# Two chunks interleaved at every second head, and four PSUM banks evacuated one by one, in an attention + FFN kernel on eight cores

## The reference

```python
x = x + layernorm(attention(layernorm(x)))
x = x + layernorm(ffn(layernorm(x)))

# attention, 16 heads of 64, linear, causal, in chunks
q, k, v = split(x @ w_qkv.T + b_qkv)
qf, kf = features(q), features(k)   # normalise, project, square, exp, clip
kv_cum = cumsum(kf * v) + carry ; k_cum = cumsum(kf) + carry
out = (qf . kv_cum) / max(qf . k_cum, 1e-6) @ w_out.T + b_out

# ffn: block diagonal up projection per head (4) and rail (64), then a dense one
y = einsum('btri,hrij->bthrj', x.reshape(b, t, 64, 16), rail_maker)
z = einsum('bthrj,hrkj->bthrk', y, rail_up_proj)
out = gelu(z.reshape(b, t, 16384)) @ w_cproj.T
```

## Time and profile before

| | |
|---|---|
| two runs, median | 4231.64 us (4229.14 and 4234.13) |
| the profiled execution | 4233.17 us |
| its span on the slowest core (core 6) | 4231.6 us |
| spans of the eight cores | 4181.5 to 4231.6 us |
| PE busy | 2215.4 us (52%) |
| DVE busy | 902.6 us (21%) |
| ACT busy | 943.3 us (22%) |
| granted TensorE clock, mean | 0.716 of full speed |
| main chunks of attention | about 799 to 2168 us |
| FFN, from its first layernorm | about 2240 us to the end |

### The profile page before, as it was taken

How to read it: one execution, slowest core, us unless ns; L and a number is a source line. 1 busy time by engine, 2 the same in 40 slices (tenths; PEclk the granted TensorE clock), 3 DMA queues, 4 the chain that set the end, 5 groups by cost and what they waited for, 6 DMA issues and landing times.

```text
span 4231.6 us, 30294 instructions; the slowest of 8 cores (4181.5 to 4231.6 us)
## 1 busy us (share of the span) xinstructions
PE 2215.4 (52%) x10260; PEld 1005.3 (24%) x10368; DVE 902.6 (21%) x1526; ACT 943.3 (22%) x1313; POOL 51.5 (1%) x73
## 2 busy tenths in 40 slices
PE   0334334444445444445445666667762866666664
PEld 0222222222222322223121222222221222222222
DVE  0222222233333233332343000000005100000003
ACT  0222323322322233232202111111102211111111
POOL 1000000000000000000000000000000000000000
PEclk9666666666656666666556788888885888888887
DMA  8000000000000000000002222211223022222221
GB/s 168 5 5 10 5 10 1 1 0 0 1 0 1 0 1 0 0 1 1 0 7 40 40 40 40 34 31 23 33 40 80 1 40 40 40 40 40 40 40 40
DMA packets 55077, 99.55 MB, mean 24 GB/s; under 512 B 2368, under 2 KB 18880, under 8 KB 53824
## 3 DMA queue, kind: packets, MB, share of 16 engines
q0 software_dynamic: 44880, 80.82, 12.1%
q1 hardware_dynamic: 10048, 16.79, 1.3%
HBM read 170.03 MB, written 8.39 MB: 42 GB/s over the span
## 4 chain that ended last, share of the span: by engine, by line
PE 48%; DVE 19%; ACT 12%; DMA 12%; issue 7%; DVEq 1%; ACTq 1%; POOL 0%; SPq 0%; POOLq 0%
PE psB L803 24%; DMA wc<-wcT 9%; PE psA L396 6%; PE psA L766 4%; PE psA L429 3%; DVE oacc L821 3%; DVE railsM L528 2%; DMA xa_bf<-x_carry 2%; DVE pn_bf L346 1%; DVE f32s L319 1%; PE psA L272 1%; PE psB L601 1%; PE psA L339 1%; ACT qk_bf L406 1%; ACT f32s L323 1%
## 5 line engine op out<-in xcount | busy, mean ns | idle before, releaser
L803 PE MATMUL psB<-hsl,wc 128*128 128x512 bf16 x4004 | 1048.5, 405 | 566.3 <-DMA wc<-wcT 439.0
L803 PEld LDWEIGHTS psB<-hsl,wc 128*128 128x128 bf16 x4096 | 376.5, 102 | 1105.7 <-issue 782.4
L777 ACT ACTIVATE hsl<-psA 128x512 bf16<-128x512 f32 x512 | 305.7, 597 | 1360.2 <-PE psA L766 1356.0
L821 DVE TENSOR_TENSOR oacc<-oacc,psB 128x2048 f32<-128x2048 f32 x56 | 128.1, 2288 | 1446.6 <-PE psB L803 1446.6
L396 PE MATMUL psA<-ln_bf,wqkv_bf 128*128 128x256 bf16 x1536 | 248.6, 339 | 84.5 <-DVEq L83 56.3
L266 PE MATMUL psA<-xa_bf,allones_bf 128*128 128x256 bf16 x256 | 58.3, 406 | 371.6 <-DMA xa_bf<-x_carry 211.0
L766 PE MATMUL psA<-ln,railsM 32*128 32x512 bf16 x512 | 210.1, 413 | 24.5 <-DVEq L83 13.8
L396 PEld LDWEIGHTS psA<-ln_bf,wqkv_bf 128*128 128x128 bf16 x1536 | 182.8, 121 | 146.5 <-issue 92.0
L339 PE MATMUL psA<-qk_bf,omega_bf 64*64 64x256 bf16 x384 | 50.9, 412 | 211.5 <-DVEq L83 211.5
L262 ACT ACTIVATE sq_bf<-xa_bf 128x2048 bf16<-128x2048 bf16 x32 | 61.1, 1909 | 443.2 <-DVEq L83 284.2
L429 PE MATMUL psA<-wqkv_bf,ln_bf 128*128 128x512 bf16 x496 | 137.4, 439 | 38.8 <-ACTq L83 20.6
(11 more groups left out here) (150 smaller groups left out, 2028.7 us busy)
## 6 DMA issues: line engine op xcount, KB each, us to landing
wc<-wcT POOLq DMA_DIRECT2D x32, 2048.0 KB, 17.9
x_sb<-x_own SPq DMA_DIRECT2D x8, 1024.0 KB, 23.6
y_out<-oacc SPq DMA_DIRECT2D x8, 1024.0 KB, 4.4
wqkv_bf<-wqkvT POOLq DMA_DIRECT2D x8, 768.0 KB, 47.9
xa_bf<-x_carry POOLq DMA_DIRECT2D x8, 512.0 KB, 5.9
wout_bf<-woutT POOLq DMA_DIRECT2D x8, 256.0 KB, 67.1
rut_bf<-rut POOLq DMA_DIRECT2D x4, 128.0 KB, 5.7
omega_bf<-omega POOLq DMA_DIRECT2D x2, 128.0 KB, 15.3
```

The source lines that it names most:

```text
L777: A_((lambda a, fcl=fcl, zsl=zsl, hb=hb: a.activation(hb[:, fcl * 512:(fcl + 1) * 512], psA[:, zsl * 512:(zsl + 1) * 512], AF.Gelu)), wait ...
L803: t.matmul(psB[:, ob * 512:(ob + 1) * 512], wcbufs[fcl // 8][:, (fcl % 8) * 1024 + obi * 128: (fcl % 8) * 1024 + (obi + 1) * 128], hb[:, f ...
L821: V_((lambda v, g=g, obg=obg: v.tensor_tensor(AP(oacc, obg * 4096 + g * 512, [[8 * 1024, 128], [1024, 4], [1, 512]]), AP(oacc, obg * 4096 ...
```

## The change

Two edits. In stage B, `pump()` is called at every second head instead of every third: 8 times in the head loop instead of 6. In the FFN, the evacuation of `psB` is cut into four operations of 512 columns, one for each bank, and a bank's first matmul waits for the operation on its own bank only (`evac_dv`). Lines behind the second edit move by up to 5: L766 becomes L767, L803 L805, L815 L818 and L821 L825.

```diff
             for hh in range(H):
-                if hh % 3 == 0:
+                if hh % 2 == 0:
                     pump()
...
             wc_sem = [emit_wc_load(0), emit_wc_load(1)]
+            evac_dv = [P.snap("dv")] * 4
...
                     for obg in range(2):
-                        dv_guard = P.snap("dv")
+                        dv_guard = list(evac_dv)
...
                                 w = []
-                                if fcl == 0 and ob == 0:
-                                    w = [("ac", h_done_for[i]),
-                                         ("dwc", max(wc_sem)),
-                                         ("dv", dv_guard)]
+                                if fcl == 0:
+                                    w = [("dv", dv_guard[ob])]
+                                    if ob == 0:
+                                        w += [("ac", h_done_for[i]),
+                                              ("dwc", max(wc_sem))]
...
-                        else:
-                            V_((lambda v, g=g, obg=obg: v.tensor_tensor(
-                                AP(oacc, obg * 4096 + g * 512,
-                                   [[8 * 1024, 128], [1024, 4], [1, 512]]),
-                                AP(oacc, obg * 4096 + g * 512,
-                                   [[8 * 1024, 128], [1024, 4], [1, 512]]),
-                                AP(psB, 0, [[2048, 128], [512, 4], [1, 512]]),
-                                op=ALU.add)), waits=[("pe", pm)])
...
+                        for ob in range(4):
...
+                            else:
+                                V_((lambda v, g=g, obg=obg, ob=ob: v.tensor_tensor(
+                                    AP(oacc, (obg * 4 + ob) * 1024 + g * 512,
+                                       [[8 * 1024, 128], [1, 512]]),
+                                    AP(oacc, (obg * 4 + ob) * 1024 + g * 512,
+                                       [[8 * 1024, 128], [1, 512]]),
+                                    psB[:, ob * 512:(ob + 1) * 512],
+                                    op=ALU.add)), waits=[("pe", pm)])
+                            evac_dv[ob] = P.snap("dv")
                     if g == 1:
                         wc_free_dv[0] = P.snap("dv")
                         wc_free_dv[1] = P.snap("dv")
```

More of the change, by code:

```diff
@@ L813, in build_nc @@
                             hsl_free[i % 2] = pm
-                        if grp == 0:
-                            V_((lambda v, g=g, obg=obg: v.tensor_copy(
-                                AP(oacc, obg * 4096 + g * 512,
-                                   [[8 * 1024, 128], [1024, 4], [1, 512]]),
-                                AP(psB, 0, [[2048, 128], [512, 4], [1, 512]]))),
-                               waits=[("pe", pm), ("dout", P.snap("dout"))])
-                        else:
-                            V_((lambda v, g=g, obg=obg: v.tensor_tensor(
-                                AP(oacc, obg * 4096 + g * 512,
-                                   [[8 * 1024, 128], [1024, 4], [1, 512]]),
-                                AP(oacc, obg * 4096 + g * 512,
-                                   [[8 * 1024, 128], [1024, 4], [1, 512]]),
-                                AP(psB, 0, [[2048, 128], [512, 4], [1, 512]]),
-                                op=ALU.add)), waits=[("pe", pm)])
+                        for ob in range(4):
+                            if grp == 0:
+                                V_((lambda v, g=g, obg=obg, ob=ob: v.tensor_copy(
+                                    AP(oacc, (obg * 4 + ob) * 1024 + g * 512,
+                                       [[8 * 1024, 128], [1, 512]]),
+                                    psB[:, ob * 512:(ob + 1) * 512])),
+                                   waits=[("pe", pm), ("dout", P.snap("dout"))]
+                                   if ob == 0 else [("pe", pm)])
+                            else:
+                                V_((lambda v, g=g, obg=obg, ob=ob: v.tensor_tensor(
+                                    AP(oacc, (obg * 4 + ob) * 1024 + g * 512,
+                                       [[8 * 1024, 128], [1, 512]]),
+                                    AP(oacc, (obg * 4 + ob) * 1024 + g * 512,
+                                       [[8 * 1024, 128], [1, 512]]),
+                                    psB[:, ob * 512:(ob + 1) * 512],
+                                    op=ALU.add)), waits=[("pe", pm)])
+                            evac_dv[ob] = P.snap("dv")
                     if g == 1:
```

## The result

The changed kernel takes 4272.13 us (median of 26 runs) against 4235.29 us for the kernel before (25 runs): a ratio of 1.0081 with a 95% interval of 1.0059 to 1.0104, 34 us more. The ratio leaves out executions in which the cores of one die ran at a lower granted clock than the others and the time was some per cent longer, so it isn't the quotient of the two medians. The profiled execution took 4273.76 us, its span on the slowest core 4272.1 us.

The account below looks back on a forecast made before the run. Attention was bound by a dependency chain through the engines, the FFN by TensorE's waits for weights and VectorE. 4233.2 + 9 (moved steps) + 22 (FFN) = 4264, less 1.5 for plain runs: 4262 us, range 4215 to 4305.

Parts of the forecast that it names:

- The third term: Attention: V pass ahead of the projection, which ends at M + 15.6 (M: last head's L528): +2.75 us per chunk.
- The fifth: Attention, chunk end: VectorE no longer waits for V passes and transposes, -4.85 us per chunk; colder first head, +0.6.
- The first: Attention: the second K pass, new in the head loop, costs 2.3 us net per chunk.
- The features: Attention: K features moved from behind the bias into the head loop, 24.7 us in either place, so 0.
- The split's price in the 48 waits: FFN: last of four pieces ends 0.83 us later, each wait costs 0.19 us more: +9 us.
- The clock: FFN: clock falls stay at 28 of 32 and 5 of 16 waits: 0, bounds -58 to +38 us.
- Rival (a): FFN: three early matmuls keep the clock up, no falls: -58 us, 4204 us; chance 0.13.
- Rival (b): FFN: the broken-up wait lowers the clock at all 48 waits: +38 us, 4300 us; chance 0.14.
- The loads: FFN: 14 weight loads each start 0.83 us later and nothing hides it: +11.6 us.
- Rival (d): FFN: the weight loads' later start is absorbed: -12 us, 4250 us; chance included in the forecast's 0.58.
- Rival (c): Attention: V pass fits under head 15's tail (-2.75), layernorm matmuls run warm (-1.9): 4229 us; chance 0.12.

## Why the prediction was right, and where its terms were off

The forecast was 4262 us, 0.7% slower than 4231.6. Measured: 0.81% (0.59 to 1.04). The terms one by one.

**K passes, K features, V pass, end of the chunk.** The third term: the V pass began at M + 2.8 (1314.55 - 1311.72) and took 5.85 us, the projection ended at M + 15.8, against M + 15.6. The fifth: from the layernorm's square to the next M 12.9 us instead of 13.5, since the layernorm's matmuls now meet PE at its higher clock (1.03 us for eight instead of 1.86; the row after stands above). PE's row before:

```profile
1324.17 1.86 PE L266 MATMUL psB<-qf_a,allones_bf 128*128 128x256 bf16 x8 [8.05 <-DVEq L83]
```

The first: a K pass in the loop stretches its head to 8.3 to 8.8 us, not 8.05. Together 1.46 us per chunk, forecast 1.25; 10 us, forecast 9. The features were neutral: 29.84 us at a head, before and after. That the move hides work that was hidden already is what the chunk period shows.

**The split's price in the 48 waits: mis-sized.** The forecast took 0.12 us between two pieces and from it came to 0.19 us per wait. L609's operations, from which the 0.12 came, have no wait of their own behind the first; the pieces have one each, and a wait costs 0.07 us even when met. Measured: 0.19 us between pieces, and 16.92 - 16.54 = 0.38 us per wait. For 48 waits this is 18 us, not 9. The experiment with one wait per evacuation shows the cause (0.12 us between pieces, a shortest distance of 16.71 us, so 0.17 us per wait).

**The clock: the counts did not stay.** The forecast kept 28 and 5 falls. Over eight cores, the falls inside went from 26.8 to 19.3, those between stayed at 3.9. A fall costs 1.3 to 1.7 us, so 7.5 fewer return 10 to 13 us. Rival (a) was right in its direction and came to about a quarter of its size. It expected PE's longest idle to drop below 0.9 us; it is 1.18. The idle sum stayed, as the forecast had it (2.47 us, 2.6 forecast), and the counts fell all the same. Rival (b) is not borne out: short matmuls in the pause made the falls fewer. By the Trainium skill ("TensorE: Matmul & The Clock Gate", "A second HAM failure mode: psum-queue depth-cycling") short idles between groups of matmuls make the clock swing; here four short ones made it swing less than the one of 2.57 us they replaced. The two errors, +9 and about -12, nearly cancel, and that is luck: the mean distance inside is 17.83 instead of 17.87, between 23.06 instead of 22.66, 32 x (-0.04) + 16 x 0.40 = +5 us, where the forecast had +9.

**The loads.** The forecast gave 14 x 0.83 us. The last piece ended 1.02 us later. The mean distance at a load grew by 0.5 us in this profile. It varies by over 1 us between profiles of kernels that all have the split (53.1 to 54.6), so it alone doesn't decide. The loads by PE's matmul do: an earlier start counts in full. Rival (d) falls. With 14 x 1.02 = 14 and 2 us at the two ends, 5 + 16 = 21 us for the FFN, forecast 22; the runs of the split alone say 11 and 29. The profile itself has less, 5 + 7 + 2 = 14 us per core.

**Rival (c)** had its warm layernorm matmuls, 0.6 us of them, but the V pass did not fit under the head's tail.

**The sum.** That 31 us forecast meet 34 measured is in part luck. In the profiles the mean span of the eight cores grew by 24 us (4206 to 4231), 10 in attention and 14 in the FFN, and in the repeat by 23. The slowest core has the rest: in the profile it grew by 40 us, 23 of them in its wait for the weights, which in the mean over the cores grew by 2. How far the slowest core lies behind the mean varies without the change too, from 17 to 25 us between the three sets of runs of the kernel before.

What stays open: whether the split makes the slowest core fall further behind or chance did; and why the passes run slower when the projection comes first.

## What to carry to other kernels

Cutting an evacuation into pieces releases the first bank early, but the consumer that needs all banks again within its first four matmuls waits for the last piece, and that one is later by the fixed cost and the gap of each extra operation. What removes such a wait is a second set of banks: two pairs that alternate gave 4.5% with the same matmuls, 5.3% with the weight loads tied to their real last reader as well, and 7.7% when each half of the weights was also loaded and awaited by itself. Before moving steps between stages, ask whether the place they leave was hidden already.

## What the runs showed of the hardware

- A VectorE operation with a wait that was already met starts 0.19 us behind the one before it, one without a wait 0.12 us (0.875 against 0.81 us from start to start of 0.69 us pieces).
- A pause of 2.57 us in a dense row of matmuls was followed by a fall from 2.4 to 1.2 GHz 26.8 times in 32; with the pause broken by three matmuls into four of 1.18, 0.29, 0.50 and 0.50 us, 19.3 times; with nine matmuls in the pause not once on six of eight cores, and 7 times in 32 on the other two.
- A weight load issued 2.5 us earlier on all eight cores brought 3.2 us per load, so the shared memory did not absorb it.
